# Conditional residual GEMMs in float32 on one core: a handover one sequence behind, whole loads of the fifth and sixth x, and a last step by halves

## The reference

```python
# x (32,128,2048) f32; cond (32,) in 0..15; adapter (32,) in 3..7
# w0 (16,128,128) f32;  w1 (8,2048,2048) f32
x = x + einsum('bct,bcd->bdt', x, w0[cond])        # per sequence, over its 128 channels
x = x + einsum('bsi,boi->bso', x, w1[adapter])     # per sequence, over its 2048 columns
```

## Time and profile before

| | |
|---|---|
| timed runs, median of 3 | 1509.91 us (1509.09 to 1510.62) |
| profiled execution | 1513.23 us |
| its span (first to last instruction) | 1511.4 us |
| mean granted clock of TensorE | 0.997 of full |
| PE busy | 1491.4 us, 99% |
| POOL busy | 1073.6 us, 71% |
| DVE busy | 1023.0 us, 68% |
| ACT busy | 512.9 us, 34% |
| HBM read, written | 227.56 MB, 33.55 MB |

### The profile page before, as it was taken

How to read it: one execution, slowest core, us unless ns; L and a number is a source line. 1 busy time by engine, 2 the same in 40 slices (tenths; PEclk the granted TensorE clock), 3 DMA queues, 4 the chain that set the end, 5 groups by cost and what they waited for, 6 DMA issues and landing times.

```text
span 1511.4 us, 28973 instructions
## 1 busy us (share of the span) xinstructions
PE 1491.4 (99%) x6564; PEld 1231.8 (82%) x6565; DVE 1023.0 (68%) x647; ACT 512.9 (34%) x788; POOL 1073.6 (71%) x655
## 2 busy tenths in 40 slices
PE   7999999999999999999999999999999999999998
PEld 5788888888888888888888888888888888888886
DVE  7783977958671679786675277976859419788511
ACT  3423333333333333333333333333333333333332
POOL 3566877768776788776777577767778767787663
PEclk9999999999999999999999999999999999999999
DMA  8795999979795699897988478988889758898443
GB/s 182 169 223 136 214 196 193 207 157 210 155 192 120 150 204 184 182 201 162 189 178 181 116 166 184 208 183 182 185 175 191 157 121 182 183 204 182 116 119 78
DMA packets 290982, 261.34 MB, mean 173 GB/s; under 512 B 19096, under 2 KB 211608, under 8 KB 290968
## 3 DMA queue, kind: packets, MB, share of 16 engines
q10 hardware_dynamic: 113376, 173.59, 49.8%
q1 hardware_dynamic: 177592, 87.60, 31.4%
HBM read 227.56 MB, written 33.55 MB: 173 GB/s over the span
## 4 chain that ended last, share of the span: by engine, by line
PE 95%; DVE 1%; issue 1%; SPq 1%; ACTq 1%; DMA 1%; POOL 0%; ACT 0%; DVEq 0%
PE z_ps L828 30%; PE z_ps L820 30%; PE z_ps L819 30%; PE out_ps L840 2%; PE out_ps L837 2%; PE out_ps L838 2%; SPq L216 1%; DMA x_nat<-in_x 1%; DVE w_low L671 0%; POOL w_low L311 0%; DVE x_turn L664 0%; DVE w_low L687 0%; ACTq L216 0%; DMA ids_row<-in_itok_B 0%; ACTq L209 0%
## 5 line engine op out<-in xcount | busy, mean ns | idle before, releaser
L820 PE MATMUL z_ps<-w_low,x_high 128*128 x1984 | 772.8, 390 | 1.0 <-issue 1.0
L819 PE MATMUL z_ps<-w_high,x_high 128*128 x1984 | 772.7, 389 | 0.0
L288 POOL TENSOR_TENSOR x_low<-x_turn,x_high 128x1024 fp32r<-128x1024 f32 x244 | 617.5, 2552 | 24.6 <-ACT x_high L361 24.5
L653 DVE STREAM_TRANSPOSE x_turn<-x_nat 128x1024 f32<-128x1024 f32 x246 | 290.8, 1219 | 424.4 <-DMA x_nat<-in_x 424.2
L828 PE MATMUL z_ps<-w_high,x_low 128*128 x1984 | 470.4, 389 | 0.0
L820 PEld LDWEIGHTS z_ps<-w_low,x_high 128*128 128x128 f32 x1984 | 372.9, 188 | 78.9 <-issue 1.4
L828 PEld LDWEIGHTS z_ps<-w_high,x_low 128*128 128x128 f32 x1984 | 372.9, 188 | 77.6
L819 PEld LDWEIGHTS z_ps<-w_high,x_high 128*128 128x128 f32 x1984 | 372.9, 188 | 77.4
L294 POOL TENSOR_TENSOR z_low<-z_raw,z_high 128x512 fp32r<-128x512 f32 x127 | 168.2, 1325 | 219.4 <-ACT z_high L368 219.3
L376 ACT ACTIVATE out_sb<-out_ps 128x512 f32<-128x512 f32 x128 | 76.5, 597 | 606.7 <-PE out_ps L840 577.1
L361 ACT ACTIVATE x_high<-x_turn 128x1024 fp32r<-128x1024 f32 x248 | 251.6, 1061 | 41.9 <-DVE x_turn L653 33.3
(11 more groups left out here) (105 smaller groups left out, 316.4 us busy)
## 6 DMA issues: line engine op xcount, KB each, us to landing
x_nat<-in_x ACTq DMA_DIRECT2D x492, 256.0 KB, 5.2
w_nat<-in_L_cond_weight SPq DMA_DIRECT2D x316, 256.0 KB, 7.5
out<-out_sb ACTq DMA_DIRECT2D x128, 256.0 KB, 5.1
a_full<-in_L_cond_weights ACTq DMA_DIRECT2D x128, 64.0 KB, 5.2
x_nat<-in_x SPq DMA_DIRECT2D x68, 64.0 KB, 2.5
x_nat<-in_x ACTq DMA_DIRECT2D x28, 64.0 KB, 3.5
w_nat<-in_L_cond_weight ACTq DMA_DIRECT2D x6, 128.0 KB, 3.8
w_nat<-in_L_cond_weight SPq DMA_DIRECT2D x2, 128.0 KB, 4.8
```

The lines of the kernel that those rows point to most:

```text
L288: nc.gpsimd.tensor_tensor(x_low[s][:, half], x_turn[:, half], x_high[s][:, half], ALU.subtract)\
L653: nc.vector.transpose(x_turn[:].rearrange("p (k a c) -> p k a c", a=QUAD, c=SQ)[:, blocks], x_nat[:].rearrange("p (a k c) -> p k a c", a=Q ...
L819: nc.tensor.matmul(z_ps[s][:], xs, w_high[:, ds(at + k * NC, NC)], start=(k == 0), stop=False)
L820: nc.tensor.matmul(z_ps[s][:], xs, w_low[:, ds(at + k * NC, NC)], start=False, stop=False)
```

## The change

1. **x4 and x5** are loaded by `load_sequence` on SP: four transfers of 256 KB each. x4 waits until all 16 ramp quarters are turned (`xq_turned` 16), x5 until both halves of x4 are turned. DVE turns both with `turn_x(RAMP + i, 0)`; `turn_x_by_quarters` is gone. `x_loaded` starts lower by two sequences, since SP's loads now count on it.
2. **The handover is one sequence behind.** On PE, the last piece of step s is followed by `by_a(s-1)`; `by_a(3)` stands in the middle of step 4's high passes. On ACT the drain of a step comes behind the copies of the next z; the rounding of x4 behind the drain of step 0; the rounding of x5 and the load of x6 behind the store of step 2.
3. **The last step by halves.** Step 127 keeps its two halves of 256 columns in PSUM tiles of their own (`z_ps[2]`, `z_ps[3]`; results in `z_ps[0]`, `z_ps[1]`). The first half's low pass, copy, `by_a`, drain (ACT) and store (ACT's queue) run ahead of those of the second, whose drain is on DVE and whose store is on SP's queue.

```diff
 # SP
-            for i in range(AHEAD):
-                b = by_step(sp, SEQ, RAMP + i, B - 1)
-                for m in range(PIECES):
-                    if i == 0:
-                        sp.wait_ge(xq_turned, (PIECES - 1) * RAMP + m + 1)
-                    else:
-                        sp.wait_ge(x_turned, 2 * (RAMP + i - 1) + m // 2 + 1)
-                    load_x_quarter(sp, m, m, b, FORTH)
+            sp.wait_ge(xq_turned, PIECES * RAMP)
+            load_sequence(sp, by_step(sp, SEQ, RAMP, B - 1))
+            b = by_step(sp, SEQ, RAMP + 1, B - 1)
+            sp.wait_ge(x_turned, 2 * (RAMP + 1))
+            load_sequence(sp, b)
...
+            store_end(sp, 1, by_step(sp, RESULT, STEPS - 1, B * P * T - NC) + NC // 2)
 # ACT
-            act.sem_inc(x_loaded, (RAMP + AHEAD) * QUAD * DMA)
+            act.sem_inc(x_loaded, RAMP * QUAD * DMA)
...
             take_z(0, 0)
-            take_x(4, 0)
-            at = evict(0, 0, None)
+            act.wait_ge(out_made, 1)
             take_a(1, 1)
             take_z(1, 1)
+            at = evict(0, 0, None)
+            take_x_half(4, 0, 0)
+            take_x_half(4, 0, 1)
             store(0, 0, at)
             act.wait_ge(a_split, 2)
             load_a(3, 1)
-            take_x(5, 1)
-            load_x(6)
-            at = evict(1, 1, None)
+            act.wait_ge(out_made, 2)
             take_a(2, 0)
             take_z(2, 2)
+            at = evict(1, 1, None)
             store(1, 1, at)
             act.wait_ge(a_split, 3)
             load_a(4, 0)
-            at = evict(2, 0, 1)
+            act.wait_ge(out_made, 3)
             take_a(3, 1)
             take_z(3, 3)
+            at = evict(2, 0, 1)
             store(2, 0, at)
+            take_x(5, 1)
+            load_x(6)
...
-            take_z(STEPS - 1, 1, raw=False)
-            store(STEPS - 1, 1, evict(STEPS - 1, 1, STEPS // 2 - 1))
+            for h in range(2):
+                act.wait_ge(gemm_done, STEPS + 1 + h)
+                nc.scalar.activation(z_high[:, END[h]], end_z_ps[h][:, END[h]], COPY).then_inc(z_copied, 1)
+            at = by_step(act, RESULT, STEPS - 1, B * P * T - NC)
+            act.wait_ge(out_stored[1], (STEPS // 2 - 1) * DMA)
+            act.wait_ge(out_made, STEPS)
+            nc.scalar.activation(out_sb[1][:, END[0]], end_out_ps[0][:, END[0]], COPY).then_inc(end_copied[0], 1)
+            store_end(act, 0, at)
 # DVE
+                dve.wait_ge(xq_split, PIECES * RAMP)
                 for i in range(AHEAD):
-                    turn_x_by_quarters(i)
+                    turn_x(RAMP + i, 0)
                     low_x(i)
...
+            for h in range(2):
+                dve.wait_ge(z_copied, 2 * STEPS - 1 + h)
+                nc.vector.tensor_tensor(z_low[:, END[h]], end_z_ps[h][:, END[h]], z_high[:, END[h]], ALU.subtract)\
+                    .then_inc(z_split, 1)
+            dve.wait_ge(out_stored[1], (STEPS // 2 - 1) * DMA)
+            dve.wait_ge(out_made, STEPS + 1)
+            nc.vector.tensor_copy(out_sb[1][:, END[1]], end_out_ps[1][:, END[1]]).then_inc(end_copied[1], 1)
 # PE
             for s in range(RAMP):
-                if s == RAMP - 1:
-                    by_a(0, 2)
                 ramp_piece(PIECES - 1, s).then_inc(gemm_done, 1)
+                if s > 0:
+                    by_a(s - 1, 2 * s)
             q, at = of_step(RAMP)
-            high_passes(RAMP, 0, q, at, 0, KP)
-            by_a(1, 4)
-            high_passes(RAMP, 0, q, at, KP, 3 * KP)
-            by_a(2, 6)
-            high_passes(RAMP, 0, q, at, 3 * KP)
+            high_passes(RAMP, 0, q, at, 0, 2 * KP)
+            by_a(RAMP - 1, 2 * RAMP)
+            high_passes(RAMP, 0, q, at, 2 * KP)
             low_pass(RAMP, 0, at)
-            by_a(3, 8)
...
-            step(STEPS - 1, 1)
-            by_a(STEPS - 1, 2 * STEPS - 1)
...
+                xs = x_high[1][:, k * P:(k + 1) * P]
+                for ws in (w_high, w_low):
+                    for h in range(2):
+                        nc.tensor.matmul(end_z_ps[h][:, END[h]], xs, ws[:, ds(at + (k * NC + h * NC // 2), NC // 2)],
+                                         start=(k == 0 and ws is w_high), stop=False)
+            by_a(t - 1, t * 2)
...
+            end_low_pass(0, 0, KB).then_inc(gemm_done, 1)
+            end_low_pass(1, 0, 3 * KP)
+            end_by_a(0)
+            end_low_pass(1, 3 * KP, KB).then_inc(gemm_done, 1)
+            end_by_a(1)
```

More of the change, by code:

```diff
@@ L165, in build, with store_end @@
         out_stored = [sem(f"out_stored{s}") for s in range(2)]
+        end_copied = [sem(f"end_copied{h}") for h in range(2)]
+        end_stored = [sem(f"end_stored{h}") for h in range(2)]
         ramp_high = [x_high[0][:], x_high[1][:]] + [w_high[:, WBUF + s * T:WBUF + (s + 1) * T] for s in (2, 3)]
         ramp_low = [x_low[0][:], x_low[1][:]] + [w_low[:, WBUF + s * T:WBUF + (s + 1) * T] for s in (2, 3)]
+        END = [slice(h * NC // 2, (h + 1) * NC // 2) for h in range(2)]
+        end_z_ps, end_out_ps = z_ps[2:], z_ps[:2]
         block = ctx.enter_context(nc.Block())
+        def store_end(eng, h, at):
+            eng.wait_ge(end_copied[h], 1)
+            eng.dma_start(bass.AP(out.tensor, at, [[T, P], [1, NC // 2]]), out_sb[1][:, END[h]])\
+                .then_inc(end_stored[h], DMA)
+            eng.wait_ge(end_stored[h], DMA)
         def by_step(eng, row, t, most, tab=step_tab):
@@ L354, in load_a, with take_x_half @@
                     .then_inc(a_loaded[s], DMA)
+            def take_x_half(t, s, h):
+                half = slice(h * T // 2, (h + 1) * T // 2)
+                act.wait_ge(x_turned, t * 2 + (h + 1))
+                nc.scalar.activation(x_high[s][:, half], x_turn[:, half], COPY).then_inc(x_high_made, 1)
             def take_x(t, s):
                 for h in range(2):
-                    half = slice(h * T // 2, (h + 1) * T // 2)
-                    act.wait_ge(x_turned, t * 2 + (h + 1))
-                    nc.scalar.activation(x_high[s][:, half], x_turn[:, half], COPY).then_inc(x_high_made, 1)
+                    take_x_half(t, s, h)
             def take_z(t, s, raw=True):
@@ L505, in _ @@
             beside(STEPS - 1, 1, STEPS // 2 - 1, more=False)
-            take_z(STEPS - 1, 1, raw=False)
-            store(STEPS - 1, 1, evict(STEPS - 1, 1, STEPS // 2 - 1))
-            for s in range(2):
-                act.wait_ge(out_stored[s], STEPS // 2 * DMA)
+            for h in range(2):
[6 more added lines that the diff above has]
+            store_end(act, 0, at)
+            act.wait_ge(out_stored[0], STEPS // 2 * DMA)
         @block.vector
@@ L623, in turn @@
                 return nc.vector.transpose(turned[:, r0:r1], nat[:, r0:r1])
[L625 to L637, removed]
             def low_x(i):
@@ L783, in _ @@
             turn_ahead(last_start, STEPS - 1)
-            dve.wait_ge(z_copied, 2 * STEPS - 1)
-            nc.vector.tensor_tensor(z_low[:], z_ps[1][:], z_high[:], ALU.subtract).then_inc(z_split, 1)
+            for h in range(2):
[5 more added lines that the diff above has]
+            nc.vector.tensor_copy(out_sb[1][:, END[1]], end_out_ps[1][:, END[1]]).then_inc(end_copied[1], 1)
         @block.tensor
@@ L926, in _, with end_low_pass, end_by_a @@
                 step(2 * p + 2, 0)
-            step(STEPS - 1, 1)
-            by_a(STEPS - 1, 2 * STEPS - 1)
+            t = STEPS - 1
+            q, at = of_step(t)
+            for k in range(KB):
+                if k % (KB // 2) == 0:
+                    pe.wait_ge(x_high_made, t * 2 + (1 + 2 * k // KB))
+                if k % KP == 0:
+                    pe.wait_ge(w_ready, q * PIECES + (k // KP + 1))
+                xs = x_high[1][:, k * P:(k + 1) * P]
[4 more added lines that the diff above has]
+            by_a(t - 1, t * 2)
+            def end_low_pass(h, first, end):
+                for k in range(first, end):
+                    if k % (KB // 2) == 0:
+                        pe.wait_ge(x_split, t * 2 + (1 + 2 * k // KB))
+                    last = nc.tensor.matmul(end_z_ps[h][:, END[h]], x_low[1][:, k * P:(k + 1) * P],
+                                            w_high[:, ds(at + (k * NC + h * NC // 2), NC // 2)],
+                                            start=False, stop=(k == KB - 1))
+                return last
+            def end_by_a(h):
+                pe.wait_ge(a_split, t + 1)
+                pe.wait_ge(z_copied, 2 * t + (1 + h))
+                nc.tensor.matmul(end_out_ps[h][:, END[h]], a_high[:], z_high[:, END[h]], start=True, stop=False)
+                nc.tensor.matmul(end_out_ps[h][:, END[h]], a_low[:], z_high[:, END[h]], start=False, stop=False)
+                pe.wait_ge(z_split, t + (1 + h))
+                nc.tensor.matmul(end_out_ps[h][:, END[h]], a_high[:], z_low[:, END[h]], start=False, stop=True)\
+                    .then_inc(out_made, 1)
+            end_low_pass(0, 0, KB).then_inc(gemm_done, 1)
[3 more added lines that the diff above has]
```

(1 more changed line is left out.)

## The result

The changed kernel's timed runs have a median of 1514.8 us (6 runs, 1513.38 to 1516.3); the old kernel's beside them 1510.3 us (6 runs, 1509.09 to 1511.39). The ratio is 1.0026, 95% interval 1.0016 to 1.0036: slower by 3.9 us, where 2.0 us less was forecast. The profiled execution took 1514.73 us around a span of 1512.9, so it stands at the median. That of the old kernel, 1513.23, stood 2.9 us above its own. From profile to profile the change therefore costs 1.5 us.

What follows compares the result with a forecast made beforehand. PE was taken as the bound (99% busy), leaving only the handover to improve: 4.3 us won at step 5, 1.7 left at step 8, plus 0.3 in the last step, 2.0 off 1509.91 gives 1507.9 us; range 1504.3 to 1512.4.

Steps and rivals of the forecast that it cites:

- 1.7 us are left of the 4.3: At step 8: of 4.3 us won at step 5, 1.7 remain, since x8 moves its start only from 117.1 to 115.4.
- x8 as the next bound: At step 8: PE, early at step 5, waits for x8, whose first half is rounded at 115.4; idle time 2.5 us.
- 10.25 us as before: Producers' chain before step 8: x7, issued at 84.7, takes 10.25 us as in the old kernel, until 95.0.
- 7.1 us are lost: Old handover from ramp to steady steps: PE loses 7.1 us, 3.7 of idle time and 3.4 from the clock's fall.
- PE starts step 8 at 117.10: Old profile's step 8: start at 117.10, with x8's first half rounded at 114.9, so 2.2 us of slack.
- x4 as a whole: Handover: x4's whole load gives a first transpose at 59.4 and a stall of 2.6 to 2.8 us at `by_a(2)`.
- Step 5 at 78.1: End of the handover: PE reaches step 5 at 78.1 instead of 82.42, so 4.3 us are won there.
- one idle time near 3.5 us: PE's waits: the clock falls near the end of 3.56 us of idle time, not at a wait of 0.8 us.
- The second piece: Next weights' second piece: lands at 89.7 (before 83.89), prepared until 96.0, so x7 is turned from 96.0 instead of 95.47.
- The last step by halves: 0.3 us won: Step 127: shorter chain behind z against 0.35 us more matmul spacing; 0.3 us won, bounds 0.8 won and 0.7 lost.
- the clock falls while PE waits for x8: Rival at step 8's start, chance 0.12: a clock fall costs 3.4 us; 1513.0, or 1511.3 with x8 at 115.4.
- No gain, without a fall of the clock: Rival at step 8, chance 0.15: x8 slips by 2 more, step 8 near its old time, 1509.5 to 1511.

Runs made afterwards that it cites:

- e4: The changed kernel with the last step whole, as in the old one: median 1512.88 us, ratio 1.0014 to the old kernel.
- e6: The changed kernel with PE's read of step 4's table entry put ahead of the ramp's last pieces: median 1514.74 us, ratio 1.0027 to the old kernel.
- e7: The changed kernel without SyncE's wait for x6 ahead of the second weight piece: median 1513.06 us, ratio 1.0014 to the old kernel.
- e2: The old kernel with only the last step by halves: median 1512.31 us, ratio 1.0004 to the old kernel.
- e9: The changed kernel with x8 turned by DVE ahead of the fourth weight piece: median 1511.54 us, ratio 1.0003 to the old kernel.
- e12: The old kernel with x8 turned by DVE ahead of the fourth weight piece: median 1511.53 us, ratio 1.0002 to the old kernel.
- e8: The old kernel with only the whole loads of x4 and x5, old order, last step whole: median 1516.15 us, ratio 1.0031 to the old kernel.
- e3: The old kernel with only the handover's new order on PE and ACT, x4 and x5 by quarters: median 1509.35 us, ratio 0.9993.
- e5: The old kernel with the new handover order and PE's table read ahead of the ramp's last pieces: median 1510.92 us, ratio 0.9999.
- e1: The old kernel once more, unchanged: median 1511.37 us, ratio 1.0001.
- e10: The changed kernel with both the early table read and x8 turned ahead of the fourth weight piece: median 1511.66 us, ratio 1.0007.

## Why the prediction was wrong

**What is to be explained.** 2.0 us were to be won and 3.9 were lost: 5.9 us. Profile to profile the change lost 1.5 us, so 3.5 of the 5.9 lie in the working itself and some 2.4 in the execution that it started from. In the two profiles the 3.5 are in two places. Step 9 is at 129.10, 0.4 us later than the old kernel's 128.66, where 1.7 us were to be won: 2.1 us. From step 9 to step 127 both take 1364.08 us. From there to the end the changed kernel takes 19.7 us and the old one 18.7, where 0.3 were to be won: 1.4 us.

**The step that failed** is the sum's "1.7 us are left of the 4.3" at step 8. The mechanism was right, x8 as the next bound; x7's term in it, "10.25 us as before", measured 12.2, and the copies that ACT makes behind x8 were not in the sum at all. What follows takes the terms one by one.

**The baseline.** The prediction subtracted from one profiled execution, and read in it "7.1 us are lost" and "PE starts step 8 at 117.10". Four traces of the old handover have step 8 at 117.1, 117.5, 114.7 and 114.7; four of the changed one (the changed kernel, e4, e6, e7) at 116.9, 116.8, 116.2 and 116.5. Against the late old executions the new step 8 is up to 1.3 us early, against the others 1.4 to 2.1 late. The early ones are early throughout: in e2 x8's first half is rounded at 112.4, so the slack of over 2 us that the prediction read was there too. The prediction gave the difference of 3.3 us between profile and median and then carried its gain over it unchanged; it ought to have asked where those 3.3 us were. This made the loss larger; but from its own late execution, too, the change lost 1.5 us, so the sign was wrong without it.

**x4 as a whole: right.** First transpose 59.0 (59.4 predicted), `by_a(2)` at 65.31 (its drain was predicted for 65.4), x6's issue at 73.57 (73.5). PE itself came later than the predicted 63.07, so its idle time at `by_a(2)` was 1.4 us and not 2.6 to 2.8.

**Step 5 at 78.1: wrong, 81.34.** Two terms were missing. The table read uncovered behind `by_a(2)` took 1.5 us, and the clock fell behind the two idle times together, which cost 1.7 us (13.29 us from step 4's first matmul to step 5's, against 11.56). The prediction asked for one idle time near 3.5 us. A third term hid behind these two: a3 landed at 69.2, later than the 68 that the prediction named as the limit for `by_a(3)`. Without the read and the fall step 8 was only 0.7 us earlier, and the time was the same (e6).

**x8 as the next bound: right, and mis-sized.** First half rounded 116.6, not 115.4, and step 8 at 116.86. The second piece came sooner than the estimate (87.9, not 89.7). But x7 took 12.2 us from issue to turning (85.09 to 97.25), not 10.25, beside the weight pieces that SyncE had issued behind each other (twelve transfers from 81.12 to 94.46). That the weights made it slow was not tried by itself. The second piece was no bound; its cast took 1.23 us with GpSimd idle, and that of the third piece, beside GpSimd's low halves of x7, 3.34. The Trainium skill's rule (SBUF — State Buffer, "Who interferes with whom"), by which VectorE and GpSimd can shut each other out, held for both casts, by this trace. That this chain carries most of the loss is shown by e9 (3.4 us back in the times, 1.5 to 2.5 in the traces) with e12 as its control; e6, which freed PE ahead of it and won nothing, agrees.

**A second wait at step 8.** ACT is parked on x8 when it ought to copy z of step 7; so `by_a(7)`'s third matmul comes late, and step 9 is at 129.10, 12.24 us behind step 8 instead of 11.56. That is 0.7 us more. The prediction followed x and the weights, and not what is queued behind `take_x` in the loop.

**The last step by halves: 0.3 us won, in fact 0.4 lost.** The chain behind z was sized rightly (0.38, 0.42, 0.42 against 0.4, 0.42, 0.42). The spacing wasn't: 0.117 was taken from matmuls whose addresses are constants. In the last step the weights' addresses come from registers and two tiles alternate, 0.132 for 64 of them, +1.0 us. The low passes take theirs from registers as well and kept 0.12, so that alone is not the cause; the alternation was not tried. The step was also counted from 1494.0 where it started at 1492.74: the "issue" gap of 1.0 us had been read over. In the changed kernel's profile it was 1.3 us, so the gap makes 0.3 of the 1.4 above.

**The parts add up, which proves little.** Halves +0.4 (trace; times 1.0004), order -1 (0.9993), loads +4.7 (1.0031): 4.1 against 3.9 measured. But e8 loses its 4.7 us at `by_a(2)`, a wait that the new order shortens, and not behind x8, so that the sum comes out is in part luck. Of the rivals, "the clock falls while PE waits for x8" came nearest in time and was wrong in kind: the clock stayed at 1.00 at step 8 in every trace. "No gain, without a fall of the clock" had the place right, step 8 near its old time; its time, 1509.5 to 1511, left out what the last step and the baseline cost.

## What to carry to other kernels

A profiled execution is one draw. Where it stands 2 or 3 us off the median, find the stretch that differs before subtracting from it: a gain worked out from a late draw may be one that most executions already have. And a stall that is removed hands over to the slowest producer: move the item that PE needs next (here one transpose of 2.4 us) ahead of work that isn't due, and check the edit on both kernels. The larger transfers were no gain here, where the small ones were pipelined with the engine that frees and reads the buffer (e8).

## What the runs showed of the hardware

- TensorE's granted clock fell to its lower level after idle times of 1.43 and 1.47 us with three matmuls between them, and after 0.20 and 1.66 us in e3; it stayed up after 1.35 and 1.44 us in the same place in e9, after 1.99 us in e6, and after 3.07 us in one piece in e5. With the same code up to there it fell in the changed kernel and did not in e9.
- A table read by PE's sequencer costs 1.4 to 1.7 us where a wait has emptied the queue (the changed kernel, e3, e4, e7, e9), and nothing where matmuls are queued ahead of it (e5, e6).
- A whole x took 12.2 us from issue to turning beside twelve transfers of weights (x7 in the changed kernel), and 7.4 us in the earlier trace rows.
- A cast of 128x2048 on VectorE took 1.23 us with GpSimd idle and 3.34 beside a subtraction of GpSimd, in one trace.
- 256-column matmuls followed each other by 0.132 us in the last step's high passes and by 0.12 in its low passes.
- In the last step an "issue" gap of 0.7 to 1.3 us comes and goes: seven traces have it (the old and the changed kernel's, e1, e4, e5, e10, e12), seven don't. It stands behind the loop's end; its cause stays open, and it is one part of the spread between executions.
- Eleven executions of one kernel on one chip spread over 2.6 to 4.7 us, so that a part worth 1 us is told by its trace and not by its times.
